# Three half-precision passes for the hidden-state gate products, a shorter early count, and a later wait for the last store, in a graph-attention kernel

## What is computed

```python
h = relu(layernorm(x))                       # 8192 x 128
Wh = h @ W
e = leaky_relu(Wh @ a_src + (Wh @ a_dst).T, 0.2)
att = softmax(where(adj > 0, e, -9e15), axis=1)
h_prime = att @ Wh
gi = h_prime @ w_ih.T + b_ih                 # 384 columns: r, z, n
gh = h @ w_hh.T + b_hh                       # 384 columns: r, z, n
r = sigmoid(i_r + h_r); z = sigmoid(i_z + h_z)
n = tanh(i_n + r * h_n)
x = x + (1 - z) * n + z * h
h = relu(layernorm(x))                       # second layer
x = x + adj @ (h @ W1.T + b1)
```

## Time and profile before

| what | us |
|---|---|
| median of 3 runs | 1576.88 |
| lowest, highest | 1576.55, 1579.28 |
| the profiled execution | 1577.86 |
| its span in the trace | 1576.0 |
| first matmul of the first sweep | 62.1 |
| first matmul of the second sweep | 1115.5 |
| last matmul of the second sweep ends | 1568.0 |

### The profile page before, as it was taken

One profiled execution on the slowest core, in us unless ns is written; L12 is line 12 of the kernel. 1 busy time (PEld: TensorE's weight loads), 2 busy tenths in 40 slices (PEclk: granted clock), 3 DMA queues, 4 the chain that ended last, 5 costly groups with the idle time before them and its releaser, 6 DMA issues.

```text
span 1576.0 us, 35430 instructions
## 1 busy us (share of the span) xinstructions
PE 1508.2 (96%) x13356; PEld 1333.0 (85%) x13388; DVE 1364.9 (87%) x2161; ACT 1350.7 (86%) x1952; POOL 135.3 (9%) x96
## 2 busy tenths in 40 slices
PE   5468999999999999999999999999999999999997
PEld 4357888888888888888888888888888888888887
DVE  8898999999999999999999999997479977666684
ACT  5789999999999999999999999997175898875463
POOL 5100010001000110011000100010000000000000
PEclk9788999999999999999999999999999999999999
DMA  8859999999999999999999999997276999864430
GB/s 311 296 214 362 346 351 355 348 343 348 358 350 349 341 356 346 353 335 355 347 350 340 358 349 350 343 349 286 116 312 237 401 374 363 320 256 163 178 128 16
DMA packets 96085, 486.68 MB, mean 309 GB/s; under 512 B 9432, under 2 KB 38690, under 8 KB 75042
## 3 DMA queue, kind: packets, MB, share of 16 engines
q1 hardware_dynamic: 78322, 444.54, 75.4%
q10 hardware_dynamic: 17712, 41.49, 6.9%
HBM read 402.07 MB, written 83.92 MB: 308 GB/s over the span
## 4 chain that ended last, share of the span: by engine, by line
PE 93%; DVE 4%; ACT 1%; DMA 1%; issue 1%; DVEq 0%; ACTq 0%
PE ACC L970 56%; PE ACC L1055 28%; PE GP L999 2%; PE GP L1000 2%; PE GQ L1018 1%; ACT M L491 1%; PE GP L1001 1%; DVE TB L703 1%; DVE JK L612 1%; DVE AE L698 1%; DVE JK L698 1%; DMA h_columns<-AE 1%; DVE M L629 0%; PE TG L983 0%; PE TG L1007 0%
## 5 line engine op out<-in xcount | busy, mean ns | idle before, releaser
L970 PE MATMUL ACC<-TB,M 128*128 128x258 f16 x8192 | 928.1, 275 | 38.1 <-DVE M L721 31.0
L970 PEld LDWEIGHTS ACC<-TB,M 128*128 128x128 fp8e4 x8192 | 805.0, 98 | 143.6 <-issue 39.3
L491 ACT ACTIVATE M<-SB,dsteep 128x256 fp8e4<-128x256 f32 x1304 | 533.9, 504 | 0.0
L501 ACT ACTIVATE JK<-X 128x3584 uint8<-128x3584 uint32 x124 | 395.1, 3186 | 0.0
L662 DVE TENSOR_SCALAR Y<-X 128x4096 fp8e4<-128x4096 f32 x128 | 292.2, 2283 | 28.9 <-DMA X<-in_adjb_dram 28.4
L577 ACT ACTIVATE TB<-TB 128x8192 uint8<-128x8192 fp8e4 x32 | 225.0, 7030 | 102.8 <-DVE TB L847 90.6
L1055 PE MATMUL ACC<-WG,X 128*128 128x256 f16 x2048 | 225.5, 273 | 0.0
L1055 PE MATMUL ACC<-WG,TB 128*128 128x256 f16 x2048 | 225.4, 273 | 0.0
L1055 PEld LDWEIGHTS ACC<-WG,TB 128*128 128x128 fp8e4 x2048 | 200.4, 98 | 23.2
L1055 PEld LDWEIGHTS ACC<-WG,X 128*128 128x128 fp8e4 x2048 | 200.3, 98 | 23.1
L713 DVE TENSOR_SCALAR M<-SB,nd 128x256 fp8e4<-128x256 f32 x744 | 205.6, 346 | 0.0
(11 more groups left out here) (142 smaller groups left out, 784.8 us busy)
## 6 DMA issues: line engine op xcount, KB each, us to landing
X<-in_adjb_dram SPq DMA_DIRECT2D x128, 2048.0 KB, 9.7
mask_bytes<-Y SPq DMA_DIRECT2D x128, 512.0 KB, 5.9
M<-in_adjb_dram ACTq DMA_DIRECT2D x19, 2048.0 KB, 11.7
X<-mask_bytes SPq DMA_DIRECT2D x16, 2048.0 KB, 9.3
TB<-mask_bytes SPq DMA_DIRECT2D x16, 2048.0 KB, 9.0
M<-in_xb_dram SPq DMA_DIRECT2D x8, 512.0 KB, 8.3
h_rows<-M SPq DMA_DIRECT2D x8, 512.0 KB, 4.2
R<-in_xb_dram SPq DMA_DIRECT2D x32, 128.0 KB, 6.7
```

The costliest lines, as they stand in the source:

```text
L491: ins = nc.scalar.activation(rows(mask1(c), jj), SB[u][:, :], ACT.Sigmoid, scale=STEEP, bias=dsteep[:, j:j + 1], saturate=False)
L501: nc.scalar.activation(junk[:, 0:SEEN], X[c % 2][:, 0:SEEN].bitcast(u32), ACT.Sign, accum_out=nz[:, bass.ds(k, 1), at:at + 1].rearrange("p ...
L970: ins = nc.tensor.matmul(A[t][m][:, 0:2 * TW], rows((mask1, mask2)[m](c), jj)[:, t * P:(t + 1) * P], TB[:, c * JC + jj, m, 0:2 * TW], star ...
```

## The change

**Gates.** The h half of the gates no longer uses f32. The rows HT of a block are rounded by DVE to f16 (HH, part 0), and the rest is kept as a second f16 part (HH, part 1). The weights whhT become two f16 parts as well, prepared on POOL together with w_ih in one tile GW. PE then does three f16 passes over 384 columns (high by high, high by low, low by high) where it did an f32 product of 256 columns and one of 128. The gate columns are reordered to n of x, r, z, n of h, so that both products write 384 neighbouring columns. DVE's `gated` becomes `gate_step`, with the two halving instructions interleaved with the two old ones.

**Count.** SEEN falls from 7/8 to 13/16 of a chunk. The second sweep counts the last 3/16 of 124 chunks, five chunks a load, so 25 loads in place of 16 (LATE = 4 + 25 in place of 4 + 16). The tally becomes one sum over all counts.

**Last store.** SP's wait for the output stores leaves the block ahead of the barrier and stands behind the branch (and inside it, if it is taken).

**Prelude.** Two small memsets on POOL, one more transfer each on SP and on ACT, the bias sum on five rows; SP waits for POOL's weight preparation ahead of its first block, since the raw weights now lie in R, which the blocks use.

The diff, cut to its core:

```diff
-SEEN = JC * RW * 7 // 8
+SEEN = JC * RW * 13 // 16
+GROUP = 5
-LATE = CS + NS // 2
+LATE = CS + 25
...
+        for u in range(2):
+            nc.sync.wait_ge(q_out[u], NS // 2 * 16)
...
+                sp.wait_ge(p_bias, 12)
                 each_row_block(sp, slot, 1)
...
-                for u in range(2):
-                    sp.wait_ge(q_out[u], NS // 2 * 16)
...
-                pool.wait_ge(wt_in, 48)
-                nc.gpsimd.tensor_scalar(wihf, wihf, WSCALE, None, ALU.mult).then_inc(p_bias, 1)
-                nc.gpsimd.tensor_scalar(whhT[:, :], whhT[:, :], WSCALE, None, ALU.mult).then_inc(p_bias, 1)
-                pool.wait_ge(p_bias, 8)
-                nc.gpsimd.tensor_copy(wihT[:, 0, :], wihf).then_inc(p_bias, 1)
+                pool.wait_ge(wt_in, 64)
+                nc.gpsimd.tensor_scalar(wraw, wraw, WSCALE, None, ALU.mult).then_inc(p_bias, 1)
+                pool.wait_ge(p_bias, 9)
+                nc.gpsimd.tensor_copy(GW[:, 0, :, :], wrawv).then_inc(p_bias, 1)
                 pool.wait_ge(p_bias, 10)
-                nc.gpsimd.tensor_tensor(wihT[:, 1, :], wihf, wihT[:, 0, :], ALU.subtract).then_inc(p_bias, 1)
+                nc.gpsimd.tensor_tensor(GW[:, 1, :, :], wrawv, GW[:, 0, :, :], ALU.subtract).then_inc(p_bias, 1)
...
-                        first, last = max((n - CS) * 2 * CS, CS), (n - CS + 1) * 2 * CS
+                        first = CS + (n - CS) * GROUP
+                        last = min(first + GROUP, NS * CS)
...
+                def gate_step(qh, u, n, q):
+                    halving, gating = qh is not None, q is not None
+                    if halving:
+                        dve.wait_ge(g_in[u], (n + 1) * 48)
+                        wait(dve, g_b, qh)
+                        dve.sem_inc(turn, 1)
+                        nc.vector.tensor_copy(HH[:, 0, :], HT[u]).then_inc(d_hh, 1)
+                    if gating:
...
+                    if halving:
+                        dve.wait_ge(d_hh, qh + 1)
+                        nc.vector.tensor_tensor(HH[:, 1, :], HT[u], HH[:, 0, :], ALU.subtract).then_inc(d_hl, 1)
...
-                    pe.wait_ge(g_in[u], (n + 1) * 48)
+                    pe.wait_ge(d_hl, q + 1)
...
-                        nc.tensor.matmul(bank[:, 0:2 * F], h_t, whhT[:, 0:2 * F], start=False, stop=False)
-                        ins = nc.tensor.matmul(bank[:, 3 * F:4 * F], h_t, whhT[:, 2 * F:3 * F], start=False, stop=True)
+                        for left, part in ((h_t, 0), (h_t, 1), (h_l, 0)):
+                            ins = nc.tensor.matmul(bank[:, F:4 * F], left, GW[:, part, 1, :], start=False,
+                                                   stop=(left is h_l))
```

More of the change, by code:

```diff
@@ L64, in graph_layers, with binary_adjacency @@
         redo = outer.enter_context(nc.sbuf_tensor("redo", [1, 1], mybir.dt.int32))
-        binary_adjacency(nc, sem, redo, xb, adjb, w, wt, a, wiht, whht, b_ih, b_hh, w1t, b1, out)
+        q_out = [sem(f"q_out{b}") for b in range(2)]
+        binary_adjacency(nc, sem, q_out, redo, xb, adjb, w, wt, a, wiht, whht, b_ih, b_hh, w1t, b1, out)
         needed = nc.values_load(redo[0:1, 0:1], min_val=0, max_val=1)
         with nc.If(needed != 0):
+            for eng in (nc.sync, nc.scalar, nc.vector, nc.tensor, nc.gpsimd):
+                for u in range(2):
+                    eng.wait_ge(q_out[u], NS // 2 * 16)
             any_adjacency(nc, outer, xb, adj, w, a, w_ih, w_hh, b_ih, b_hh, w1, b1, out)
-def binary_adjacency(nc, sem, redo, xb, adjb, w, wt, a, wiht, whht, b_ih, b_hh, w1t, b1, out):
+        for u in range(2):
+            nc.sync.wait_ge(q_out[u], NS // 2 * 16)
+def binary_adjacency(nc, sem, q_out, redo, xb, adjb, w, wt, a, wiht, whht, b_ih, b_hh, w1t, b1, out):
     ctx = ExitStack()
@@ L97, in binary_adjacency @@
         h2T = sb("h2T", [P, RW])
-        wihT = sb("wihT", [P, 2, 3 * F], f16)
-        whhT = sb("whhT", [P, 3 * F])
+        GW = sb("GW", [P, 2, 2, 3 * F], f16)
+        HH = sb("HH", [P, 2, RW], f16)
         w1T = sb("w1T", [P, F])
@@ L161, in binary_adjacency @@
         brow = TBf[0:5, 0:2 * F].bitcast(f32)
-        bhid = TBf[0:2, 2 * F:4 * F].bitcast(f32)
+        bhid = TBf[0:5, 2 * F:4 * F].bitcast(f32)
         bres = [TBf[0:5, (4 + 2 * k) * F:(6 + 2 * k) * F].bitcast(f32) for k in range(2)]
@@ L995, in gates @@
                         a_t, a_l = [hpT[:, part, t * F:(t + 1) * F] for part in range(2)]
-                        h_t = HT[u][:, t * F:(t + 1) * F]
+                        h_t, h_l = [HH[:, part, t * F:(t + 1) * F] for part in range(2)]
                         nc.tensor.matmul(bank, onesb[:, :], BI[:, 0:4 * F], start=True, stop=False)
                         for left, part in ((a_t, 0), (a_t, 1), (a_l, 0)):
-                            nc.tensor.matmul(bank[:, 0:3 * F], left, wihT[:, part, :], start=False, stop=False)
-                        nc.tensor.matmul(bank[:, 0:2 * F], h_t, whhT[:, 0:2 * F], start=False, stop=False)
-                        ins = nc.tensor.matmul(bank[:, 3 * F:4 * F], h_t, whhT[:, 2 * F:3 * F], start=False, stop=True)
+                            nc.tensor.matmul(bank[:, 0:3 * F], left, GW[:, part, 0, :], start=False, stop=False)
+                        for left, part in ((h_t, 0), (h_t, 1), (h_l, 0)):
+                            ins = nc.tensor.matmul(bank[:, F:4 * F], left, GW[:, part, 1, :], start=False,
+                                                   stop=(left is h_l))
                     ins.then_inc(g_b, 1)
@@ L1087, in sums @@
                     pe.wait_ge(k_df, 4)
-                    nc.tensor.matmul(GP[:, 0:NS // 2], ones[:, :], odd[:, :, 0:1].rearrange("p g o -> p (g o)"), start=True,
-                                     stop=True)
+                    nc.tensor.matmul(GP[:, 0:1], ones[:, :], odd[:, 0:1], start=True, stop=True)
                     nc.tensor.matmul(GP[:, P:2 * P], ones[:, :], tmp[:, 0, :], start=True, stop=True).then_inc(k_w, 1)
```

80 lines of the change are left out of this document (45 added, 35 removed).

## The result

| what | us |
|---|---|
| before, median of 4 runs | 1576.72 (1575.62 to 1579.28) |
| after, median of 4 runs | 1563.91 (1562.82 to 1564.71) |
| ratio of the two | 0.9916, 95% interval 0.9899 to 0.9933 |
| profiled execution of after, its span | 1564.71, 1563.0 |

The changed kernel is 12.8 us faster; 12.2 were forecast. The two spans differ by 13.0 us.

A forecast was written before the change was run, and what follows sets the result against it. PE was taken as the bound, with ACT, DVE and DMA close behind. Gates 10.2, start 0.6 and end 1.35 sum to 12.2 us off the median of 1576.88: 1564.7 us, with an 8-in-10 range of 1562.0 to 1568.5.

The forecast's parts named there:

- The bound: Steady blocks: PE bounds, busy 510.84 of 511.68 us; ACT, DVE and the DMA engines are 2 to 6% behind.
- The gates: PE's gate step: three f16 passes replace the f32 part, 0.16 us less in each of 64 halves, 10.2 us.
- The start and the end: Block 1 starts 0.6 us earlier after three shorter counts; redo loads 1.35 us earlier without the store wait.
- The clock: PE's chunks up to 139 us run partly at the lower clock; its rise may move 1 or 2 us either way.
- DVE, 0.6 a block: Two halving instructions in DVE's gate step add 0.6 us a block (0.49 to 1.06), fitting within the 31.66 us period.
- ACT and the loads: Shorter count: ACT loses 0.84 us a block, X is freed earlier, DVE waits less for loads; steady time unmoved by itself.
- The rival of the loads as a bound: At 349 GB/s loads hold the period at 31.98 us; only start and end gain, 1574.9 us; chance 0.06.
- The late count: Second sweep: nine more loads and counts cost nothing, with 3.3 us of cover left behind the last tally instruction.
- 12 us and more of cover: Rival that the late count ends too late or the prelude holds SP; this cover must vanish first; chance 0.02.
- The prelude: POOL's weight preparation takes 3.6 us more, ending about 47.2, with 6.7 us of cover for SP: cost 0, at most 0.5.
- the slow rival: DVE becomes the bound if rounding costs 1.74 us a block: 1579 us, up to 1590; chance 0.04.
- point of decision: DVE has 1.3 us a block for the new pair before the gain shrinks, 1.6 before the kernel is slower.

The follow-up runs named there:

- two-pass run: The changed kernel without the third gate pass over h (low part of h by high part of w_hh), a rougher result: 1553.0 us, ratio 0.9851.

## Why the prediction was right

**The bound.** Read right: TensorE's path, with every other engine behind it. The run with the gates alone takes 0.33 us off the period with the count and the store's wait as before, and the two-pass run takes off another 0.33.

**The gates, 10.2 forecast.** 10.56 measured. The step was right, and its size is the rounding of 0.65 - 0.49: rows of 10 ns resolution give 0.16, the periods give 0.33 for two halves.

**The start and the end, 0.6 and 1.35.** 0.64 and 1.35. Both stand in the trace of the kernel without the new gates too.

**The clock.** I allowed 1 or 2 us either way; it gave 0.49. That part of the gain was in no term of the sum.

**DVE, 0.6 a block.** 0.40. It was mis-sized from above and even lies under my low bound of 0.49: I took 0.26 for the rounding from six instructions of another shape, and it took a step of 0.20, while the subtraction between the old pair took 0.33 and the pair's own gap shrank from 0.45 to 0.33. The Trainium skill's rule (VectorE: DVE Perf Modes, the perf-mode tier table) of a single-source f32 copy at twice the rate of a two-tensor operation was weighed there, and the direction holds, at 0.20 against 0.33 us a step, but at 256 columns that is 1.65 times and not twice. The prediction called 0.26 against 0.34 an agreement; that was 1.3 times, from instructions with another output type. Busy time went from 30.4 to 30.8 us a block, where 31.0 was forecast. The runs with two and five more subtractions show that neither would have changed the time.

**ACT and the loads.** ACT lost 31.53 - 30.76 = 0.77 us a block (0.84 forecast). DVE's wait for loads fell as said. The rival of the loads as a bound is out: the two-pass kernel drew 356 GB/s in the same loop.

**The late count.** Priced at nothing, with 3.3 us of cover behind the tally; it cost nothing and 3.4 were left (1545.2 to 1548.62). The rival's "12 us and more of cover" does not fit the prediction's own 3.3 here and 6.7 for SP in the prelude; the 3.3 was the right one.

**The prelude.** POOL's end was forecast at 47.2 and came at 42.2, ahead of the old 43.6: a wrong term without effect. The rows show why. Before, POOL's rounding of 384 columns took 2.61 us; now the one of 768 takes 0.82 (timeline of POOL).

```profile
37.23 2.13 POOL L412 TENSOR_SCALAR R<-R 128x768 f32<-128x768 f32 x1
39.43 0.82 POOL L414 CAST GW<-R 128x768 f16<-128x768 f32 x1
40.34 1.65 POOL L416 TENSOR_TENSOR GW<-R,GW 128x768 f16<-128x768 f32 x1
```

The 2.61 were no price of rounding, but mostly a wait (the last section has the rows). Doubling them was the failed step, and so was taking them as the dearest row for a rounding on DVE in the slow rival.

**The slow rival's mechanism.** DVE as the bound is real once it needs more than the period; the run of five shows it. Its point of decision held (free at 0.6 more, dear at 1.7 more), but its lead was mis-sized: not 10.8 us on the masks, but 7.1 on hp, of which 4.2 were there when it began to shrink steadily, and 2.4 on ACT's second evacuation. I had looked at the masks only, since they stand in TensorE's large line.

## What to carry to other kernels

Where one engine is busy for all of a period, an edit on it can be priced from two neighbouring rows to a tenth of a microsecond; what needs care is the engines behind it, and those are priced by the busy time a block and by the lead on each thing that the bound takes from them, from the first blocks on, not by the most frequent one in a steady block. An engine's idle stretch ahead of a block is not all to be had: moving a release forward gains only up to the next product that must be ready, and an instruction that is put back to make room also puts back the load queued behind it.

## What the runs showed of the hardware

**DVE and POOL hold each other up.** In the kernel before, DVE's `ones_of` ran 39.64 to 42.03 and POOL's rounding, begun at 39.77, ended at 42.38. In the changed kernel POOL was first, and now DVE's 128-column instructions are stretched: the six take 4.07 us instead of 2.01, one of them 1.81 us, ending at 42.06, with POOL's subtraction (41.99). The timeline of DVE before, then after:

```profile
37.89 2.01 DVE L629 TENSOR_SCALAR M<-M,JK 128x128 f32<-128x128 f32 x6
39.64 2.39 DVE L662 TENSOR_SCALAR Y<-X 128x4096 fp8e4<-128x4096 f32 x1
```

```profile
37.99 4.07 DVE L642 TENSOR_SCALAR M<-M,JK 128x128 f32<-128x128 f32 x6
41.99 2.38 DVE L675 TENSOR_SCALAR Y<-X 128x4096 fp8e4<-128x4096 f32 x1
```

DVE lost 2.35 us there and had them back in a wait for ACT. The Trainium skill states it as a lock (SBUF — State Buffer, Who interferes with whom): copies, casts and `tensor_scalar` of DVE in a two-port mode and GpSimd share a port pair, and whoever begins first holds it for the whole instruction. The trace agrees, in both directions, as far as POOL's rows, which are rough, can tell. No run here was made for it, so it rests on these rows.

**The clock where block 1 starts.** The kernels with the evacuations behind the mask and with the count behind them make a pair: block 0's last 64 matmuls took 9.78 and 9.76 us in them, at a granted clock of 0.73 in both. Then one idled for 3.3 us, and its first 128 matmuls of block 1 took 17.08 us at 0.83. The other idled for 0.4 us, and they took 14.24 us at 1.00, which is also what 128 of them take in the middle of the sweep. In the changed kernel they took 16.28 behind 7.3 us. So an idle stretch there cost 2 to 3 us more than its own length. These are single executions, and I did not find a rule for where the clock rises.

**Memory.** The stretch from 1215 to 1265 us in the second sweep moved 407 GB/s where it had been 378, with TensorE without a gap in both: this core was not held to 378.
